# Neighbour sums and sort written out step by step, sums between the last node products, ten tiles of the first normalisation on ScalarE

## The chip, the cores and the metric

One Trainium2 chip, of which the kernel uses one core. The metric is the device time of one execution in microseconds (us), as the median of several runs; lower is better. A profiled execution stands beside it: one run of the same program taken by the hardware profiler, whose trace all rows below come from.

The engines are called by the names of the trace: PE (TensorE, matmul; PEld is its weight load), DVE (VectorE), ACT (ScalarE), POOL (GpSimd) and SP (SyncE, which only starts transfers here). Each runs its own instruction stream, in order, and waits on semaphores that the others raise. A small processor ahead of each engine, the sequencer, reads that stream: it carries out register and branch instructions itself and hands the rest to the engine's queue.

## The reference

Four updates of a node table `x` of 3,125 nodes by 256 values, each on the layer-normalised table:

```python
x = x + _L0_gnn_ref(_layernorm(x), src, dst, weight, bias)      # mean of h[src] over 50,000 edges, h = x @ W + b
x = x + _L0_ffn_ref(_layernorm(x)[None], ...)                   # graph attention on 32,768 edges picks 2 of 4 experts per node
x = x + _L1_gnn_ref(_layernorm(x), src, dst, edge_type_32, edge_weight1, bases, w_comp)   # 32 relations from 8 bases
x = x + _L1_ffn_ref(_layernorm(x)[None], Wr, br, W1, ...)       # mean of all nodes picks 2 of 8 experts, one choice for all
...
# _L1_ffn_ref: logits = jnp.mean(x, axis=1) @ Wr + br; softmax; scale by capacity; softmax; top_k; two expert MLPs; layernorm
```

All of it is float32. The last expert choice needs the mean over all nodes of the normalised table before any of its expert products can start.

## The kernel before, in words

Nodes are held as 25 tiles of 128 (`NT`), edges as 391 blocks of 128 (`EB`). The program is a row of blocks of code, one after the other.

**First normalisation and neighbour sums** (`sum_neighbours`). `normalise` (line 185) has DVE take the statistics of the 25 tiles, ACT a square root, and DVE then write all 25 normalised tiles `XN` (line 196). SP stores them to `xn_table` in five pieces of five tiles (line 603), and POOL begins to gather rows once all five have landed (line 615). Each gather (line 473) fetches the 128 source rows of one edge block; POOL keeps 16 blocks ahead of the sums at most (`LEAD_A`) and waits for PE in groups of four.

The sums run in 52 steps (`step`) of eight slots. In each step PE reads from tables in memory which ring place each slot's rows lie in and which gathers have to have landed (`registers` and `counts`, TENSOR_LOAD rows of line 123 and 131), and makes eight products of a one-hot matrix with the gathered rows (line 763) into four banks; DVE adds each bank to the node's sum (line 1148) and makes the next one-hot matrices (line 962).

Into these steps a second job is woven: a counting sort of the 32,768 attention edges. It uses whatever PE, DVE and ACT have free between the sums, and goes through four stretches:

- counting, 14 steps: written out on PE and DVE, a loop on ACT (line 674);
- two steps in which totals are made;
- bases, 5 steps (`BASED` to `PLACED`): a loop on PE (841), on DVE (1179) and on ACT (683);
- placing, 32 steps, one chunk of the sort in each (b = 0 to 31): on DVE b = 0 to 3 and 30, 31 are written out, the rest is a loop of two steps per turn (1192); on PE b = 0, 1 and b = 16, 17 are written out, b = 2 to 15 and 18 to 31 are two loops of seven turns (866, 871); on ACT b = 4 to 31 is a loop (693). Three more steps follow.

In a placing step, PE makes `equals` (781, 785), the places of the chunk before (`places_of`, 795 and 797) and the permutation of the one before that (804); ACT copies (652) and builds columns (662, 665); DVE carries values (1093), reads the places (1083 to 1088), makes tiles (1036), and at the step's end the one-hot rows of the next chunk (`hots`, line 1078), for which SP has loaded a row of digits (609). PE's `equals` of a step needs DVE's `hots` of the step before, so no engine can run more than about a step ahead.

Inside a loop the addresses and the values that a wait compares with depend on the turn, so each is worked out in registers by the sequencer; written out they are constants.

**Middle.** The update of the nodes, the attention, the experts and the sums over relations follow, none of them touched by the change.

**Last update** (`third_update`). PE makes the last four node products `z_ps` (line 2308, 16 products each); between them it turns (transposes, line 2301) the 21 tiles that are already normalised, seven after each of the first three node products (`SUMS`); ACT copies each turned tile out of one of two PSUM buffers (2269). DVE adds the products to `X` (2374), measures, and sums the turned tiles over the nodes (`node_sums`, 2369) in four groups: 7, 7, 7 and 4 tiles. The router of some 30 small DVE instructions (2398 to 2434) follows, then the transfers of the chosen experts' weights (SP, 2244), then the expert products (2330, 2342).

```python
SUMS = [range(0, 7), range(7, 14), range(14, NT - ZT), range(NT - ZT, NT)]     # line 2206, ZT is 4
```

## Time and profile before

| | us |
|---|---|
| median of 3 runs (lowest, highest) | 2281.04 (2280.89, 2281.67) |
| the profiled execution, its own time | 2285.36 |
| its span in the trace | 2283.6 |
| start to first gather | 0 to 47.33 |
| first gathers and counting | 47.33 to 212.00 |
| bases (5 steps) | 212.00 to 278.68 |
| placing and the last steps | 278.68 to 694.60 |
| node update, attention, experts | 694.60 to 1200, about |
| experts, sums over relations | 1200 to 2033, about |
| last node products and router | 2033.00 to 2092.00 |
| last experts, output | 2092.00 to 2283.60 |

Busy over the span: PE 1666.2 us (73%), DVE 1276.7 (56%), POOL 1076.5 (47%), ACT 712.2 (31%).

How to read it: start times are us from the start of the span. "issue" as a releaser means that the engine waited for nothing that the profile shows, and "remote" that what let it go has no engine's record beside it. A step's end is taken here as DVE's row of line 1078, which is made once per placing step.

### The profile page before, as it was taken

The numbers are of one execution on the slowest core, as the hardware profiler recorded it, in microseconds if no ns is written. First come the engines' busy times: TensorE is split into PE (matmuls) and PEld (weight loads), VectorE is DVE, ScalarE is ACT, GpSimd is POOL, SyncE is SP. The second block draws the span as 40 slices with busy tenths as digits, with TensorE's granted clock in tenths as the row PEclk, the third lists the DMA queues.
The fourth block names the chain that finished last, engine by engine and source line by source line (L and its number), as shares of the span: only waits on it lengthen the run. The fifth ranks groups of instructions, "written<-read, shape, count | busy, mean of one in ns | idle before, by whom it ended". The sixth has DMA issues, their size and how long they took to land. (4 is left out here: it accounts for less than half of the span.)

```text
span 2283.6 us, 32653 instructions
## 1 busy us (share of the span) xinstructions
PE 1666.2 (73%) x8780; PEld 1319.3 (58%) x8781; DVE 1276.7 (56%) x3698; ACT 712.2 (31%) x1566; POOL 1076.5 (47%) x1102
## 2 busy tenths in 40 slices
PE   2776566766777799999934646565756799996997
PEld 1444344444445577777723546555645699984786
DVE  7877777667677410222146636555656566656235
ACT  1001146555651222222204632232323233312222
POOL 1676666555660566666640065555555554300000
PEclk9987578788789799999966867777777799997999
DMA  5233233333332122232251543433333565611001
GB/s 165 78 89 92 73 98 104 96 104 103 101 97 74 29 70 70 69 91 70 76 158 8 177 129 117 133 118 118 116 112 114 166 219 197 201 37 42 0 1 57
DMA packets 165026, 226.82 MB, mean 99 GB/s; under 512 B 35764, under 2 KB 124118, under 8 KB 162070
## 3 DMA queue, kind: packets, MB, share of 16 engines
q0 software_dynamic: 47392, 105.58, 16.5%
q1 hardware_dynamic: 114176, 115.99, 15.7%
q10 hardware_dynamic: 3318, 3.59, 0.5%
q8 instruction: 63, 1.03, 0.2%
q14 instruction: 77, 0.63, 0.1%
HBM read 172.48 MB, written 105.03 MB: 122 GB/s over the span
## 5 line engine op out<-in xcount | busy, mean ns | idle before, releaser
L473 POOL DMA_INDIRECT edge_rows<-xn_table,edge_source x391 | 376.5, 963 | 402.2 <-ACT held L2111 177.6
L2123 PE MATMUL part<-coef,held 128*128 128x128 f32 x2368 | 400.8, 317 | 215.7 <-issue 181.0
L473 POOL DMA_INDIRECT shared_space<-xn_table,edge_source x391 | 402.4, 1029 | 277.8 <-issue 108.5
L2123 PEld LDWEIGHTS part<-coef,held 128*128 128x128 f32 x2368 | 371.4, 228 | 254.6 <-issue 199.3
L2161 DVE SCALAR_TENSOR_TENSOR window_sums<-window_sums,fine_keep,part 128x256 f32 x592 | 282.4, 477 | 295.9 <-remote 130.2
L763 PE MATMUL part<-shared_space,hot 128*128 x832 | 297.9, 495 | 123.9 <-issue 63.4
L2111 ACT ACTIVATE held<-edge_rows 128x256 f32 x592 | 213.9, 408 | 484.6 <-PE part L2123 228.3
L1490 POOL DMA_INDIRECT gall<-attention_table,attention_source x256 | 244.9, 957 | 132.5 <-issue 68.3
L763 PEld LDWEIGHTS part<-shared_space,hot 128*128 128x128 f32 x832 | 176.7, 239 | 194.2 <-issue 173.4
L1148 DVE TENSOR_TENSOR shared_space<-shared_space,part 128x257 f32 x416 | 174.6, 420 | 132.8 <-remote 43.5
L2148 DVE SCALAR_TENSOR_TENSOR coef<-iota,fine_target,slot_coefs 128x128 f32<-128x128 f32 x592 | 203.7, 346 | 6.8 <-PEq L1283 6.8
L1843 DVE TENSOR_TENSOR ys<-ps_of_attention,b 128x256 f32<-128x256 f32 x100 | 39.0, 419 | 299.3 <-PE ps_of_attention L1649 171.8
L1649 PE MATMUL ps_of_attention<-slot_coefs,hid 128*128 128x256 f32 x800 | 185.1, 388 | 18.5 <-DVE ys L1843 11.5
L1636 PE MATMUL ps_of_attention<-shared_space,W 128*128 128x320 f32 x640 | 181.6, 441 | 11.3 <-ACT hid L1532 8.5
L1649 PEld LDWEIGHTS ps_of_attention<-slot_coefs,hid 128*128 128x128 f32 x800 | 154.6, 194 | 47.5 <-DVE ys L1843 16.2
L2137 PE MATMUL z_ps<-bases,z 128*128 128x256 f32 x672 | 175.6, 383 | 1.3 <-issue 1.2
L1532 ACT ACTIVATE hid<-ps_of_attention,b 128x320 f32<-128x320 f32 x160 | 83.3, 527 | 266.5 <-PE ps_of_attention L1636 157.3
L1636 PEld LDWEIGHTS ps_of_attention<-shared_space,W 128*128 128x128 f32 x640 | 123.5, 194 | 64.7 <-ACT hid L1532 10.4
L662 ACT ACTIVATE sort_apart<-slot_iota,sort_col 128x256 bf16<-128x256 f32 x256 | 109.1, 496 | 45.9 <-DVEq L1089 34.1
L2137 PEld LDWEIGHTS z_ps<-bases,z 128*128 128x128 f32 x672 | 116.0, 193 | 10.3 <-issue 1.4
L2330 PE MATMUL h_ps<-XNT,V 128*128 128x320 f32 x320 | 90.1, 441 | 13.4 <-DMA V<-in_L_ffn_W 13.4
L2342 PE MATMUL y_ps<-window_sums 128*128 128x256 f32 x400 | 88.1, 379 | 0.5 <-DVE XN L2473 0.5
(467 smaller groups left out, 1926.4 us busy)
## 6 DMA issues: line engine op xcount, KB each, us to landing
basis_sums<-window_sums SPq DMA_DIRECT2D x74, 1024.0 KB
z<-basis_sums SPq DMA_DIRECT2D x21, 1024.0 KB
expert_rows<-ys SPq DMA_DIRECT2D x20, 640.0 KB
shared_space<-expert_rows SPq DMA_DIRECT2D x25, 512.0 KB, 4.7
W<-in_L_ffn_W SPq DMA_DIRECT2D x20, 512.0 KB
gall<-attention_digits SPq DMA_DIRECT2D x32, 256.0 KB
xn_table<-shared_space SPq DMA_DIRECT2D x10, 640.0 KB, 4.1
shared_space<-xn_table,edge_source POOLq DMA_INDIRECT x391
```

What stands on the lines that cost most here:

```text
L473: pool.indirect_dma_start(rows[:, b % ring, 0:D], None, table, bass.IndirectOffsetOnAxis(ap=esrc[:, b:b + 1].bitcast(U32), axis=0)).then_i ...
L662: nc.scalar.activation(apart[:, t, :], edges.slot_iota[:, 0:GT], ACT.Abs, bias=col[k][:, q * 4 + t:q * 4 + t + 1]).then_inc(apart_ready, 1)
L763: nc.tensor.matmul(part[:, n % BANKS, 0:D + 1], hot[n // HOT][:, n % HOT, :], rows[:, ds(at[n], 1), :].rearrange("p o d -> p (o d)"), star ...
L1148: V.tensor_tensor(to, to, part[:, n % BANKS, 0:D + 1], ALU.add).then_inc(added, 1)
L1490: pool.indirect_dma_start(gall[:, k, :], None, drams.table, at(att.source[:, k:k + 1])).then_inc(flights[i % FLIGHT], 16)
L1636: mm = nc.tensor.matmul(h_ps[:, n % BANKS_E, 0:HALF], W1[m % 2][:, c, f * P:(f + 1) * P], XNT[:, c, lo:lo + HALF], start=(c == 0), stop=(c ...
L1649: mm = nc.tensor.matmul(y_ps[:, (m * CT + t) % BANKS_E, :], hid[m % 2][:, f, t * P:(t + 1) * P], W2[:, m % EXPERTS, f, :], start=(f == 0), ...
L2111: nc.scalar.activation(held[k % DEEP][:, :], rows[:, ds(at[n], 1), :].rearrange("p o d -> p (o d)"), ACT.Copy).then_inc(copied, 1)
L2123: mm = nc.tensor.matmul(part[n][:, c * P:(c + 1) * P], held[n][:, c * P:(c + 1) * P], coef[n][:, :, :].rearrange("p b w -> p (b w)"), star ...
L2137: mm = nc.tensor.matmul(z_ps[:, t % 2, :], third.turned[t % AHEAD_Z][:, c * BASES + b, :], third.bases[:, b, c, :], start=(o == 0), stop=( ...
L2148: V.scalar_tensor_tensor(coef[k % DEEP][:, :, :], iota[:, 0:WIN].unsqueeze(1).to_broadcast([P, BASES, WIN]), fine.target[:, k:k + 1], coef ...
L2161: V.scalar_tensor_tensor(to, to, fine.keep[:, k:k + 1], part[k % DEEP].rearrange("p (k w) -> p k w", w=WIN), ALU.mult, ALU.add).then_inc(a ...
```

## The change

Four parts. (1) `normalise` makes tiles 0 to 14 on DVE; ACT makes tiles 15 to 24 as `x * root + off`, with `off` = minus mean times root from one more DVE instruction, and starts the stores of the last two pieces itself. (2) Every loop of the sums and the sort is written out, on PE, DVE and ACT. (3) In the last update, the turns stand singly between the 16 products of the second and the third node product, 11 and 10 of them, and `node_sums` has three groups, 11, 10 and 4 tiles; the first two are summed around the last node product's evictions. (4) In the router the comparison of indices `earlier` is made before the logits are waited for.

```diff
-    for t in range(NT):
+    link(dve.scalar_tensor_tensor(off, aggr[:, :, 0], -1.0, root, ALU.mult, ALU.mult))
+    for t in range(X_OWN):
         dve.tensor_scalar(XN[:, t, :], X[:, t, :], aggr[:, t, 0:1], root[:, t:t + 1],
...
-X_FIRST = 8
+X_FIRST, X_OWN = 8, 15
...
             for lo, hi in zip(CUTS, CUTS[1:]):
+                if hi > X_OWN:
+                    break
                 sp.wait_ge(xn_ready, hi)
...
+            act.wait_ge(xn_ready, 1)
+            for t in range(X_OWN, NT):
+                nc.scalar.activation(XN[:, t, :], X[:, t, :], ACT.Identity, bias=off[:, t:t + 1], scale=root[:, t:t + 1]).then_inc(act_made, 1)
+            for lo, hi in zip(CUTS, CUTS[1:]):
+                if lo >= X_OWN:
+                    act.wait_ge(act_made, 1 + hi - X_OWN)
+                    act.dma_start(table.rearrange("(t p) d -> p t d", p=P)[:, lo:hi, :], XN[:, lo:hi, :]).then_inc(xn_out, 16)
...
-            with act.Fori(0, PAIRS - 1) as ii:
+            for ii in range(PAIRS - 1):
...
-            with act.Fori(0, NT // CT) as w:
+            for w in range(NT // CT):
...
-            with act.Fori(2, CHUNKS_S // 2) as ii:
+            for ii in range(2, CHUNKS_S // 2):
...
-            with pe.Fori(BASED, PLACED) as i:
+            for i in range(BASED, PLACED):
                 step(i)
...
-            with pe.Fori(1, HALFWAY) as ii:
+            for ii in range(1, HALFWAY):
...
-            with pe.Fori(HALFWAY + 1, CHUNKS_S // 2) as ii:
+            for ii in range(HALFWAY + 1, CHUNKS_S // 2):
...
-            with dve.Fori(BASED, PLACED) as i:
-                link.enter(i - BASED, 2 * CT)
+            for i in range(BASED, PLACED):
                 step(i, parts=basing(i - BASED))
-                link.leave(PLACED - BASED)
...
-            with dve.Fori(2, CHUNKS_S // 2 - 1) as ii:
-                link.enter(ii - 2, 2 * PLACING)
+            for ii in range(2, CHUNKS_S // 2 - 1):
...
-        SUMS = [range(0, 7), range(7, 14), range(14, NT - ZT), range(NT - ZT, NT)]
+        SUMS = [range(0, 11), range(11, NT - ZT), range(NT - ZT, NT)]
...
-                mm.then_inc(z_ready, 1)
-                if t + ZT - NT < len(SUMS) - 1:
-                    for n in SUMS[t + ZT - NT]:
-                        turn(n)
+                    if n == len(third.products) - 1:
+                        mm.then_inc(z_ready, 1)
+                    group = t - (NT - ZT) - 1
+                    if 0 <= group < len(SUMS) - 1 and n < len(SUMS[group]):
+                        turn(SUMS[group][n])
...
+                if n == ZT - 1:
+                    node_sums(len(SUMS) - 2)
                 dve.wait_ge(z_ready, t + 1)
...
-                if 0 < n < len(SUMS) - 1:
-                    node_sums(n - 1)
+                if n == ZT - 2:
+                    node_sums(0)
...
-            for g in range(len(SUMS) - 2, len(SUMS)):
-                node_sums(g)
+            node_sums(len(SUMS) - 1)
```

What the change does to the instruction streams, at three places. Line numbers above 190 are up to ten higher in the changed program.

**PE, start of a placing step** (lines 763, 773: the sums; 795, 805 and 797, 807: the places). Before, in the loop:

```order
L758 ISA
L762 REGISTER_ALU
L763 ISA
L763 MATMUL part<-shared_space,hot 128x257
L762 REGISTER_ALU
L763 ISA
L763 MATMUL part<-shared_space,hot 128x257
L790 ISA
L795 ISA
L795 MATMUL word_ps<-sort_bases,gall 128x50
L797 MATMUL word_ps<-shared_space,edge_rel 128x25
L795 ISA
```

Now:

```order
L773 ISA
L773 MATMUL part<-shared_space,hot 128x257
L773 ISA
L773 MATMUL part<-shared_space,hot 128x257
L805 MATMUL word_ps<-sort_bases,gall 128x50
L807 MATMUL word_ps<-shared_space,edge_rel 128x25
L805 MATMUL word_ps<-sort_bases,gall 128x50
```

The register rows for the waits and for the address of each place product are gone; the row that sets the ring address of each sum stays. A placing step is 65 rows on PE before and 39 now.

**DVE, start of a placing step** (1148, 1158: the adds; 1093, 1103: the carry). Before:

```order
L1192 ISA
L123 TENSOR_LOAD coarse_tile
L1145 REGISTER_ALU
L1146 REGISTER_ALU
L1148 ISA
L1148 TENSOR_TENSOR shared_space<-shared_space,part 128x257
L1145 REGISTER_ALU
L1146 REGISTER_ALU
L1148 ISA
L1148 TENSOR_TENSOR shared_space<-shared_space,part 128x257
L1100 REGISTER_ALU
L1093 ISA
```

Now:

```order
L123 TENSOR_LOAD coarse_tile
L1158 ISA
L1158 TENSOR_TENSOR shared_space<-shared_space,part 128x257
L1158 ISA
L1158 TENSOR_TENSOR shared_space<-shared_space,part 128x257
L1103 TENSOR_SCALAR edge_norm<-sort_iota,sort_row,shared_space 128x128 x8
L1158 ISA
```

Here too only the rows that depend on data stay; a placing step is 65 rows on DVE before and 28 now.

**PE, the last node products** (2308, 2314) **and the turns between them** (2301, 2307). Before:

```order
L2308 MATMUL z_ps<-bases,window_sums 128x256 x16
L2301 MATMUL xnt_ps<-ident,XN 128x128 x14
L2308 MATMUL z_ps<-bases,window_sums 128x256 x16
L2301 MATMUL xnt_ps<-ident,XN 128x128 x14
L2308 MATMUL z_ps<-bases,window_sums 128x256 x16
```

Now:

```order
L2314 MATMUL z_ps<-bases,window_sums 128x256 x17
L2307 MATMUL xnt_ps<-ident,XN 128x128 x2
L2314 MATMUL z_ps<-bases,window_sums 128x256
L2307 MATMUL xnt_ps<-ident,XN 128x128 x2
L2314 MATMUL z_ps<-bases,window_sums 128x256
```

The three blocks of seven turns are gone, and one turn (two transposes) stands behind each single product instead.

## Rows read from the trace of the kernel before

**Rows 1.** The page, costliest groups: busy, mean ns of one, idle before:

```profile
L473 POOL DMA_INDIRECT shared_space<-xn_table,edge_source x391 | 402.4, 1029 | 277.8 <-issue 108.5
L2111 ACT ACTIVATE held<-edge_rows 128x256 f32 x592 | 213.9, 408 | 484.6 <-PE part L2123 228.3
```

**Rows 2.** Windows: length, busy of PE, PEld, DVE, ACT, POOL, PEclk, DMA, GB/s:

```profile
84.00:196.00 112.00, 81.98 (x441) 50.69 (x441) 87.42 (x173) 11.65 (x32) 82.05 (x75) 0.83 0.31 91
...
305.48:658.73 353.25, 249.49 (x1450) 173.43 (x1450) 253.32 (x755) 200.98 (x344) 209.73 (x216) 0.83 0.35 102
...
480.84:500.43 19.59, 15.70 (x100) 11.53 (x100) 17.14 (x54) 12.17 (x20) 12.26 (x13) 0.88 0.38 108
```

**Rows 3.** Waits in 300 to 692 us (POOL: 40 to 692): total, times, longest:

```profile
PE part L763 <- issue: 39.1, 38, 2.2
...
DVE shared_space L1148 <- remote: 43.2, 17, 5.8
...
POOL shared_space L473 <- PE part L763: 99.6, 38, 9.3
```

**Rows 4.** Timeline of DVE, the row that ends a placing step:

```profile
305.48 0.48 DVE L1078 TENSOR_SCALAR gall<-gall,lane 128x1024 bf16<-128x1024 bf16 x1
...
480.84 0.48 DVE L1078 TENSOR_SCALAR gall<-gall,lane 128x1024 bf16<-128x1024 bf16 x1
...
490.84 0.48 DVE L1078 TENSOR_SCALAR gall<-gall,lane 128x1024 bf16<-128x1024 bf16 x1
...
500.43 0.48 DVE L1078 TENSOR_SCALAR gall<-gall,lane 128x1024 bf16<-128x1024 bf16 x1
...
658.73 0.48 DVE L1078 TENSOR_SCALAR gall<-gall,lane 128x1024 bf16<-128x1024 bf16 x1
```

**Rows 5.** Timeline of one stall in the placing loop, PE and DVE:

```profile
403.07 0.61 PE L781 MATMUL equal_ps<-sort_earlier,sort_ident 128*128 128x512 bf16 x1 [1.91 <-issue]
...
406.18 0.99 DVE L1148 TENSOR_TENSOR shared_space<-shared_space,part 128x257 f32 x2 [5.12 <-remote]
```

**Rows 6.** Timeline of DVE, the first add of three steps of the bases loop:

```profile
236.32 0.42 DVE L1148 TENSOR_TENSOR shared_space<-shared_space,part 128x257 f32 x1 [1.45 <-issue]
...
248.02 0.42 DVE L1148 TENSOR_TENSOR shared_space<-shared_space,part 128x257 f32 x1 [1.44 <-issue]
...
268.10 0.42 DVE L1148 TENSOR_TENSOR shared_space<-shared_space,part 128x257 f32 x1 [1.44 <-issue]
```

**Rows 7.** DMA queue of instructions, whole span and 300 to 692 us: packets, MB, share:

```profile
q8 instruction: 63, 1.03, 0.2%
...
q8 instruction: 4, 0.07, 0.1%
```

**Rows 8.** Timeline of the first normalisation: start, length, engine, line:

```profile
33.59 8.16 DVE L196 TENSOR_SCALAR shared_space<-X,aggr,root 128x256 f32<-128x256 f32 x25
35.32 6.82 SPq L603 DMA_DIRECT2D xn_table<-shared_space  x5
...
47.33 1.14 POOL L473 DMA_INDIRECT shared_space<-xn_table,edge_source  x1 [44.36 <-DMA xn_table<-shared_space]
```

**Rows 9.** Timeline of the last node products:

```profile
2042.90 0.60 PE L2301 MATMUL xnt_ps<-ident,XN 128*128 128x128 f32 x4
...
2046.04 7.07 PE L2308 MATMUL z_ps<-bases,window_sums 128*128 128x256 f32 x32
...
2054.17 1.99 DVE L2369 TENSOR_REDUCE node_parts<-XNT 128x2 f32<-128x1792 f32 x1
...
2056.09 7.07 PE L2308 MATMUL z_ps<-bases,window_sums 128*128 128x256 f32 x32
...
2077.41 3.03 DVE L2369 TENSOR_REDUCE node_parts<-XNT 128x2 f32<-128x1792 f32 x2
2078.53 0.81 ACT L2269 ACTIVATE XNT<-xnt_ps 128x256 f32<-128x256 f32 x2 [0.41 <-PE xnt_ps L2301]
```

**Rows 10.** Timeline of PE, the one long wait in the written-out steps:

```profile
205.07 3.79 PE L763 MATMUL part<-shared_space,hot 128*128 x8 [5.70 <-issue]
```

More of the change, by code:

```diff
@@ L182, in measure, with normalise @@
     link.note(dve.bn_aggr(aggr[:, t, :], stats[:, t, :]))
-def normalise(dve, link, X, XN, stats, aggr, var, root, tmp, var_ready, std_ready, n, xn_ready, measured):
+def normalise(dve, link, X, XN, stats, aggr, var, root, tmp, off, var_ready, std_ready, n, xn_ready, measured):
     for t in range(measured, NT):
@@ L503, in sum_neighbours @@
         stats, aggr = edges.stats, sb("aggr0", [P, NT, 2])
-        var, root, tmp = (sb(f"{n}0", [P, NT]) for n in ("var", "root", "tmp"))
+        var, root, tmp, off = (sb(f"{n}0", [P, NT]) for n in ("var", "root", "tmp", "off"))
         ends, windows = sb("block_ends", [P, 3, EC], I32), sb("block_windows", [P, 2, 3, EC], I32)
@@ L566, in sum_neighbours @@
         xn_ready, xn_out, pads_out, digits_out = (sem(n) for n in ("xn_ready", "xn_out", "pads_out", "digits_out"))
-        src_turned, src_ready, last_ready, number_ready, start_ready = (
-            sem(n) for n in ("src_turned", "src_ready", "last_ready1", "number_ready", "start_ready"))
+        src_turned, act_made, last_ready, number_ready, start_ready = (
+            sem(n) for n in ("src_turned", "act_made", "last_ready1", "number_ready", "start_ready"))
         sel_ready, words_ready, words_used = sem("sel_ready"), sem("words_ready"), sem("words_used")
@@ L630, in _ @@
             act.wait_ge(src_turned, 1)
-            nc.scalar.activation(esrc[:, :], word_ps[:, 0, :], ACT.Copy).then_inc(src_ready, 1)
+            nc.scalar.activation(esrc[:, :], word_ps[:, 0, :], ACT.Copy).then_inc(act_made, 1)
             act.wait_ge(digits_turned, 1)
@@ L748, in _ @@
             pe.wait_ge(sel_ready, 2)
-            pe.wait_ge(src_ready, 1)
+            pe.wait_ge(act_made, 1)
             pe.wait_ge(words_used, 1)
@@ L890, in _ @@
             dve.wait_ge(edges.x_in, 16 * (NFULL // X_FIRST))
-            normalise(dve, link, X, XN, stats, aggr, var[:, :], root[:, :], tmp[:, :], var_ready, std_ready, 1, xn_ready, X_FIRST)
+            normalise(dve, link, X, XN, stats, aggr, var[:, :], root[:, :], tmp[:, :], off[:, :], var_ready, std_ready, 1, xn_ready, X_FIRST)
             dve.wait_ge(last_ready, 1)
@@ L2394, in softmax @@
                 link(V.tensor_scalar(x, sm[:, :], tmp[:, 0:1], None, ALU.mult))
+            e_of = lambda x: x.unsqueeze(2).to_broadcast([P, E8, E8])
+            o_of = lambda x: x.unsqueeze(1).to_broadcast([P, E8, E8])
+            link.note(V.tensor_tensor(earlier[:, :, :], o_of(iota[:, 0:E8]), e_of(iota[:, 0:E8]), ALU.is_lt))
             dve.wait_ge(logits_ready, 1)
@@ L2410, in _ @@
             softmax(lg[:, :], 2)
-            e_of = lambda x: x.unsqueeze(2).to_broadcast([P, E8, E8])
-            o_of = lambda x: x.unsqueeze(1).to_broadcast([P, E8, E8])
             link.note(V.tensor_tensor(larger[:, :, :], o_of(lg[:, :]), e_of(lg[:, :]), ALU.is_gt))
-            link.note(V.tensor_tensor(equal[:, :, :], o_of(lg[:, :]), e_of(lg[:, :]), ALU.is_equal))
-            link(V.tensor_tensor(earlier[:, :, :], o_of(iota[:, 0:E8]), e_of(iota[:, 0:E8]), ALU.is_lt))
+            link(V.tensor_tensor(equal[:, :, :], o_of(lg[:, :]), e_of(lg[:, :]), ALU.is_equal))
             link(V.tensor_tensor(equal[:, :, :], equal[:, :, :], earlier[:, :, :], ALU.mult))
```

3 lines of the change are left out of this document (1 added, 2 removed).

## The prediction

> **What bounds the kernel now.** The chain that ended last only reaches back over the last tenth of the span, so I read the stages by windows, then the waits, then the timeline.
>
> The stage that the change is mostly about is the placing, from 278.68 to 694.60 us. The reader is to see in its window [rows 2] that over 353.25 us no engine is full: PE 249 us, DVE 253 us, POOL 210 us. The window runs from the end of one placing step to the end of the 29th after it (305.48 and 658.73) [rows 4], so a step takes 353.25 / 29 = 12.18 us. The waits say what fills the gaps [rows 3]: 39.1 us in which PE waited for nothing the profile shows before a sum, 43.2 us in which DVE waited for "remote" before an add, and 99.6 us of POOL waiting for PE's sums. One stall shows how they hang together [rows 5]: PE idles 1.91 us before its `equals` with no releaser, and DVE's next add starts 5.12 us late.
>
> Two of these steps are different. The kernel before has placing steps b = 16 and 17 written out on PE, while DVE and ACT are inside their loops. Their ends are at 490.84 and 500.43, after 480.84 [rows 4]: 10.00 and 9.59 us, with DVE 87% busy [rows 2]. The same work costs 2.4 us less where PE's sequencer has no addresses and wait values to work out. I conclude that **PE's register work is what makes the looped steps slow**, a mechanism inferred from two steps.
>
> In the bases stage, the first adds of three successive steps stand at 236.32, 248.02 and 268.10 [rows 6]: 11.7 us for one turn of DVE's loop and 20.1 for the next, with the same instructions. The counting stage has no loop on PE or DVE. Over 112 us POOL issued 75 gathers [rows 2]; with 108.5 / 391 = 0.28 us of issue gap each [rows 1] that is 82 + 21 = 103 us of 112, so POOL bounds it.
>
> **The change part by part.**
>
> *Placing written out.* 26 rows per step go on PE, 37 on DVE. What bounds a step next? On DVE and PE together, the two written-out steps: 9.6 to 10.0 us. On POOL: 216 gathers in 29 steps [rows 2] are 7.45 per step, at (402.4 + 108.5) / 391 = 1.31 us each [rows 1], 9.7 us. Both floors lie close together, so each one's jitter falls on the other, and I take 10.2 us: 29 × (12.18 − 10.2) = 57 us. Best case 9.6 us, 75 us; the worst that a row gives is POOL at its price in the counting stage, 112 / 75 = 1.49 us, 7.45 × 1.49 = 11.1 us per step, 31 us. The last placing step and the three steps behind it, still paced by PE's loop when they start, give two more such differences: 4 us (2 to 5).
>
> *Bases written out.* The gain is the slow turn: 20.1 − 11.7 = 8.4 us [rows 6]; I take 8. It may be chance that one turn was slow, so the lower bound is 0. The 1.44 us ahead of each step's first add is a read of a table from memory, which stays.
>
> *ACT's loops written out.* ACT is 57% busy in placing (201 of 353 us [rows 2]) and 10% in counting; POOL covers it there. Nothing. If that cover went, ACT's part is the copy of the counts, off PE's path by one chunk.
>
> *More code to fetch.* The written-out stretch adds 24 placing steps' code on PE, at 1450 / 29 = 50 records each of PE and PEld [rows 2], and four bases steps: some 2,900 instructions. The whole program's 17,500 such records came in 63 packets of q8 [rows 7], which by its size is PE's queue, so 280 each; that makes 10 or 11 packets more. I cost them at nothing: the counting stage runs such code and is bound by POOL. Nearest row for a price: the longest written-out wait, 5.70 us [rows 10], though DVE's long reduction stands there too.
>
> *A rule on this point.* In 300 to 692 us q8 moved 4 packets [rows 7], while PE went 14 times through its two placing loops: the loops were not fetched anew. The Trainium skill, "Runtime: NRT & Kernel Launch", section "Instruction fetch mechanics", says that a taken branch to code outside the two pages held forces a fetch and a stall, and gives that as a reason to unroll. By this rule alone the placing loops would have at most 4 such stalls to give back, and the sum would end where the first rival does; the trace does not bear it out as the cause here.
>
> *First normalisation.* DVE's 25 tiles take 8.16 us [rows 8], 0.33 each; ten fewer and one small instruction more free DVE 3.0 us earlier. ACT makes its ten beside DVE, at 0.41 us for a 128x256 tile [rows 1]: 4.1 us from about 34.3, ready at 38.5 instead of 41.75. Behind that tile came the last store and 5.6 us to the first gather (41.75 to 47.33) [rows 8]. ACT starts two stores one behind the other after its tiles, about 1 us of that lost (SP's five take 6.8 us with their waits). First gather about 2.2 us earlier, and with POOL as the bound of counting this carries: 2.2 us (0 to 3).
>
> *Last node products.* A node product takes 7.07 us, and the next starts 10.05 us after it [rows 9]: 3.0 us for seven turns, because each pair of turns waits for ACT's copies. Three blocks: 9 us. Two turns without waits take 0.60 us on PE [rows 9], partly latency; I take 0.23 each, 21 × 0.23 = 4.8 us, the copies hidden behind the products. Gain 4.2 us (2.5 to 4.8). The turns now wait for nothing new: the 21 tiles are normalised while the first product runs. DVE's sums grow: 7 tiles 1.99 us [rows 9], so 11 and 10 take 3.1 and 2.8; with the 1.2 us of eviction and statistics ahead of them that is 7.1 us beside the last product's 7.07, so they just fit, and half a microsecond is the risk. The sum of tiles 14 to 20 leaves the end of the chain, but gains nothing: the last group's sum could only begin when ACT's last copy ended, at 78.53 + 0.81 = 79.34, and the pair ended at 80.44 [rows 9]; one sum of four tiles after 79.34 ends there too. What is late next is that copy.
>
> *Router.* One instruction of about 0.2 us leaves the chain: 0.2 us.
>
> **Sum.** 57 + 4 + 8 + 2 + 4 + 0.2 = 76 us (rounded from 57.4, 4, 8, 2.2, 4.2, 0.2). The profiled execution took 2285.36 us with a span of 2283.6, 0.19% above the median of the runs, so the difference is taken from the median: 2281 − 76 = **2205 us** (a profile of it would show about 2209). The stages behind the sums start from a common point at 694.6 and move as they are.
>
> **The rivals.**
>
> *The loops cost next to nothing, chance 0.10.* The stalls come from the tables that PE and DVE read in each step and from the landings of gathers, all of which stay; b = 16 and 17 were lucky. For it: DVE's looped and written-out steps do the same engine work. Against it: the "remote" waits stand nowhere in the written-out stretches. Time: only 2.2 + 4.2 + 0.2 are gained, 2274 us. The Trainium skill, "Advanced Engine Details and Errata", section "Control Flow Timing", gives 51 ns for a branch and 108 ns for a compare and branch; by this, 19 turns of PE's loops are an estimated 2 us, and the sum would be 2272.
>
> *POOL becomes the bound at its counting price, 0.12.* POOL's gathers took 1.09 us each where DVE was 78% busy (82.05 / 75) and 0.97 where it was 72% busy [rows 2]; a denser DVE may slow them again. 11.1 us per step: 31 + 2 + 6 + 6 = 45 us, or 2236 us.
>
> *The straight code is fetched too slowly, 0.04; slower than before.* Each of the 11 further packets holds PE up by 5.7 us [rows 10], 63 us, and everyone behind it. It decides only if the loops give back little too: 2281 − 7 + 63 = 2337 us. With my gains for the loops it would take 7 us per packet to cancel them. Against it: the placing steps 16 and 17 and the counting stage are such code.
>
> *Better than the forecast, 0.04:* all placing steps at 9.6 us or below, under 2186 us.
>
> **How the numbers follow.** The forecast has 0.70. Its best bounds together (75, 5, 8.4, 3, 4.8) reach 2185 us; the POOL rival with no gain from the bases reaches 2243. The range of 2186 to 2243 holds both cases, 0.82. Faster by over 0.2% (4.6 us, about what a measurement of this kernel can tell from no change): all cases but the fetch rival and a part of the first, 0.94. Within 0.2%: 0.02. Slower: 0.04.
>
> **What would show it.** A profile after should have placing steps 9.6 to 10.5 us apart, no "remote" waits of DVE's adds above 2 us, q8 packets up by about 11, five bases steps all near 11.7 us, the first gather near 45 us, the last node products 9.2 to 9.6 us apart with no gap of 3 us, and a placing stage of about 355 us for 416. The prediction is wrong if steps stay at 12 us (then not PE's registers), if POOL's waits for PE vanish and its gathers lengthen (POOL rival), or if PE shows waits of several us that coincide with q8 packets.

## The result, and the profile after

The changed kernel takes 2258.7 us (median of 4 runs, 2255.6 to 2259.4), the kernel before beside it 2280.97 us (2280.6 to 2281.7): ratio 0.9886, 95% interval 0.9870 to 0.9902. It is faster by 22 us where 76 were forecast, and lies outside the range of 2186 to 2243 us.

The profiled execution of the changed kernel took 2255.6 us, the fastest of its runs (that of before took 2285.4, above its own runs), so the two profiles stand 30 us apart where the medians stand 22. I therefore compare stages, and take the spread of a stage from the profiles of the experiments. Windows of the changed kernel (columns as in [rows 2]), the counting stage and 29 placing steps:

```profile
84.00:196.00 112.00, 84.16 (x436) 52.88 (x434) 89.26 (x171) 10.71 (x30) 81.73 (x76) 0.80 0.33 93
292.85:636.93 344.08, 235.68 (x1450) 165.73 (x1450) 252.63 (x755) 201.66 (x344) 209.12 (x216) 0.88 0.36 105
```

29 placing steps now take 344.08 us, 11.86 us each, where [rows 2] had 12.18 and the forecast 10.2. The waits of the same window name what stays:

```profile
PE equal_ps L791 <- ACT edge_rel L662: 51.3, 19, 4.2
ACT edge_rel L662 <- remote: 48.9, 19, 5.8
...
DVE shared_space L1158 <- remote: 38.1, 16, 5.2
POOL shared_space L474 <- remote: 34.9, 14, 2.7
```

The "remote" waits that were to vanish are there: 16 before DVE's adds, 38.1 us, against 17 and 43.2 in [rows 3], which look at a somewhat longer stretch. The other parts moved more nearly as forecast, all but the first gather. The code grew by 12 packets ([rows 7] had 63), and ScalarE made its part of the first normalisation beside VectorE:

```profile
q8 instruction: 75, 1.23, 0.2%
```

```profile
36.71 1.08 ACT L641 ACTIVATE shared_space<-X,off,root 128x256 f32<-128x256 f32 x2
36.87 2.34 DVE L197 TENSOR_SCALAR shared_space<-X,aggr,root 128x256 f32<-128x256 f32 x7
37.33 0.40 ACTq L645 DMA_DIRECT2D xn_table<-shared_space  x1
...
39.78 0.37 ACTq L645 DMA_DIRECT2D xn_table<-shared_space  x1
```

```profile
48.70 1.39 POOL L474 DMA_INDIRECT shared_space<-xn_table,edge_source  x1 [45.73 <-DMA xn_table<-shared_space]
```

VectorE is free at 39.2 us instead of 41.75, but ScalarE takes 0.51 us a tile, its last store is issued at 39.78, and the first gather comes at 48.70, later than the 47.33 of [rows 8].

In the last update the turns stand between products. VectorE's adds for the second and the third of the last four node products are 9.1 us apart, where they were 10.05 before, and the sums of 11 and 10 tiles just fit before the last one:

```profile
2026.79 0.42 DVE L2383 SCALAR_TENSOR_TENSOR X<-z_ps,X 128x256 f32<-128x256 f32 x1 [8.23 <-PE z_ps L2314]
2035.91 0.42 DVE L2383 SCALAR_TENSOR_TENSOR X<-z_ps,X 128x256 f32<-128x256 f32 x1 [8.01 <-PE z_ps L2314]
2036.93 5.78 DVE L2376 TENSOR_REDUCE node_parts<-XNT 128x2 f32<-128x2816 f32 x2
2042.81 0.42 DVE L2383 SCALAR_TENSOR_TENSOR X<-z_ps,X 128x256 f32<-128x256 f32 x1
```

**One freeze in the written-out code.** These are rows of five timelines of the changed kernel in one placing step: TensorE, SyncE, GpSimd, and ScalarE and VectorE, which wait:

```profile
302.62 0.19 PE L807 MATMUL word_ps<-shared_space,edge_rel 128*128 128x25 bf16 x1
303.39 0.39 PE L791 MATMUL equal_ps<-sort_earlier,sort_ident 128*128 128x512 bf16 x1 [0.57 <-DVE gall L1088]
303.61 0.39 PE L795 MATMUL equal_ps<-gall 128*128 128x128 bf16 x4
303.84 1.96 PE L773 MATMUL part<-shared_space,hot 128*128 x8
309.77 0.61 PE L791 MATMUL equal_ps<-sort_earlier,sort_ident 128*128 128x512 bf16 x1 [3.97 <-ACT edge_rel L662]
...
308.89 0.32 SPq L612 DMA_DIRECT2D gall<-attention_digits  x1
...
302.51 1.24 POOL L474 DMA_INDIRECT shared_space<-xn_table,edge_source  x1 [0.31 <-issue]
304.06 0.95 POOL L474 DMA_INDIRECT shared_space<-xn_table,edge_source  x1 [0.30 <-DMA shared_space<-xn_table,edge_source]
305.31 0.95 POOL L474 DMA_INDIRECT shared_space<-xn_table,edge_source  x1 [0.30 <-issue]
306.56 0.94 POOL L474 DMA_INDIRECT shared_space<-xn_table,edge_source  x1 [0.30 <-issue]
309.80 0.95 POOL L474 DMA_INDIRECT shared_space<-xn_table,edge_source  x1 [2.29 <-remote]
...
309.02 0.69 ACT L662 ACTIVATE edge_rel<-equal_ps,sort_minus 128x512 bf16<-128x512 f32 x1 [3.49 <-remote]
309.12 0.42 DVE L1158 TENSOR_TENSOR shared_space<-shared_space,part 128x257 f32 x1 [2.84 <-remote]
```

TensorE's last place product (L807) ends at 302.81. SyncE's load of the next digits waits for that product's signal alone, and is issued at 308.89, 6.1 us later. ScalarE waits for the signal of `equals`, recorded as done at 304.0, until 309.02; VectorE waits for sums recorded from 303.84 on until 309.12; the three go on within 0.25 us of each other. By its records TensorE has not stopped working: its signals are late, and come together. The semaphore records in the same trace say so directly: TensorE's updates for L807 and L795 and its next four for the sums stand at 308.87, 308.94, 308.98, 309.03, 309.07 and 309.11, while VectorE's updates are recorded all through, at 304.53 to 306.29. I call such a stretch a freeze. Meanwhile GpSimd issues four gathers one behind the other, then needs sums itself and stops at 307.50; 1.4 us later the signals come. In a step without a freeze:

```profile
353.54 0.19 PE L807 MATMUL word_ps<-shared_space,edge_rel 128*128 128x25 bf16 x1
...
353.76 0.32 SPq L612 DMA_DIRECT2D gall<-attention_digits  x1
...
351.56 0.94 POOL L474 DMA_INDIRECT shared_space<-xn_table,edge_source  x1 [0.30 <-issue]
354.32 0.94 POOL L474 DMA_INDIRECT shared_space<-xn_table,edge_source  x1 [1.82 <-PE part L773]
```

Here the signal is taken 0.03 us after the product, and GpSimd has been quiet for 1.2 us. In each of the two profiles a load of SyncE waits for 30 of the place products, and I set these 60 against the gathers around them: 14 signals came at once, and in 12 of these GpSimd's last gather had ended about 1.2 us or more before; 46 came 1.4 to 8.8 us late, and in all of these a gather was in issue or had ended at most 0.3 us before. This gave **theory A**: signals of TensorE are held while gathers follow each other without a gap, until about when the last of them has landed. The rival is the forecast's own, **F**: TensorE's register work in loops costs 2 us a step.

### The profile page after: what moved, and what is told of

Read it like the earlier page. It is cut to its first block and busy times, and to the rows that moved or that the text cites. A ratio compares the mean times of both kernels' runs of the same rounds, so it can differ in the third digit from the quotient of the medians.

```text
span 2253.8 us, 30851 instructions
## 1 busy us (share of the span) xinstructions
PE 1663.8 (74%) x8780; PEld 1321.2 (59%) x8780; DVE 1272.7 (56%) x3687; ACT 716.8 (32%) x1576; POOL 1072.9 (48%) x1102
## 5 line engine op out<-in xcount | busy, mean ns | idle before, releaser
L474 POOL DMA_INDIRECT shared_space<-xn_table,edge_source x391 | 396.3, 1013 | 261.1 <-issue 110.8
L773 PE MATMUL part<-shared_space,hot 128*128 x832 | 291.9, 492 | 107.4 <-issue 53.5
L1642 PE MATMUL ps_of_attention<-shared_space,W 128*128 128x320 f32 x640 | 187.2, 448 | 17.3 <-issue 12.6
L1655 PE MATMUL ps_of_attention<-slot_coefs,hid 128*128 128x256 f32 x800 | 178.8, 382 | 8.9 <-DVE ys L1849 7.7
L672 ACT ACTIVATE sort_apart<-slot_iota,sort_col 128x256 bf16<-128x256 f32 x256 | 109.1, 496 | 64.5 <-DVEq L1099 47.0
```

Source lines behind the costliest of these rows:

```text
L474: pool.indirect_dma_start(rows[:, b % ring, 0:D], None, table, bass.IndirectOffsetOnAxis(ap=esrc[:, b:b + 1].bitcast(U32), axis=0)).then_i ...
L773: nc.tensor.matmul(part[:, n % BANKS, 0:D + 1], hot[n // HOT][:, n % HOT, :], rows[:, ds(at[n], 1), :].rearrange("p o d -> p (o d)"), star ...
L1642: mm = nc.tensor.matmul(h_ps[:, n % BANKS_E, 0:HALF], W1[m % 2][:, c, f * P:(f + 1) * P], XNT[:, c, lo:lo + HALF], start=(c == 0), stop=(c ...
L1655: mm = nc.tensor.matmul(y_ps[:, (m * CT + t) % BANKS_E, :], hid[m % 2][:, f, t * P:(t + 1) * P], W2[:, m % EXPERTS, f, :], start=(f == 0), ...
```

## The experiments

The measure I use for a run's placing stage is the row of the digits' comparison, whose first and last start are 31 steps apart. The kernel before has 278.7 to 658.7, 380.0 us; the changed kernel 370.6:

```profile
L1088 DVE TENSOR_SCALAR gall<-gall,lane x32: 478/481/547, 266.3 to 636.9; 128x1024 bf16<-128x1024 bf16 x32
```

**The loops alone.** The kernel before with its seven loops written out, nothing else:

```diff
-            with pe.Fori(1, HALFWAY) as ii:
+            for ii in range(1, HALFWAY):
```

(and so for the six others).

> The kernel before with only its seven counted loops of the neighbour sums and the sort written out (the first normalisation and the last update as before). The changed kernel gained 22 us in all, 19 us of it by the end of the sort and 3 us in the last update. Theory A (the written-out loops brought the gain of the first stage): 2281 - 19 = 2262 us, 2259 to 2266, with a placing step near 11.9 us. Rival B (the gain of the first stage comes mostly from the first normalisation and its earlier chain of words, or from the phase in which gathers and steps meet): 2270 us or more.

Measured: 2262.1 us (2260.1 to 2268.5), ratio 0.9898 (0.9862 to 0.9934). The total is what the first of the two theories expected, but not where it comes from: the placing takes 378.3 us, almost as before. The bases take 50.9 us from first to last scan for 61.8, and 14 us lie in the edge sums (694.7 for 709.1), a stage that no part of the change touches. Over all profiles of the two kernels that stage has 687 to 709 us: the total of one kernel carries some 10 us that belong to nothing in the change.

**More and less credit for the gathers.**

```diff
-LEAD_A, LEAD_T, TURNS = 16, 16, 8
+LEAD_A, LEAD_T, TURNS = 12, 12, 8
```

(24, 24 in the second.)

> The changed kernel with both gather streams allowed to run 12 blocks ahead and not 16. Theory A (signals of TensorE that follow the place products are held while GpSimd goes on issuing gathers, and come through about 1.0 to 2.1 us after its last one, so what ends a freeze is that the gathers run out of credit): less credit ends the freezes sooner, but only if a group of four less is issued inside one; the freezes of 5.5 us (three gathers issued inside) become 2 to 4 us and the placing step falls from 11.9 to 11.0 to 11.5 us, the whole 2235 to 2255 us. Rival B (gathers that land late hold the step): less lead makes every landing later for TensorE, the step grows to 12.5 us or more and the whole to 2275 us or more. Rival C (the freeze has nothing to do with the gathers): 2256 to 2262 us.

> The changed kernel with both gather streams allowed to run 24 blocks ahead and not 16. Theory A (held until the gathers run out of credit): more credit gives longer freezes, where the stream has used it; the placing step 12.0 to 12.6 us, the whole 2262 to 2290 us. Rival B (gathers that land late hold the step): more lead removes late landings, step 10.2 to 11 us, the whole 2215 to 2240 us. Rival C (no connection): 2256 to 2262 us.

Measured: 12 ahead 2247.2 us, ratio 0.9821 (0.9789 to 0.9853); 24 ahead 2278.2 us, 0.9970 (0.9950 to 0.9990). The order is theory A's, and B (late landings) is refuted, but the mechanism was not seen: the placing takes 379.2 and 375.9 us, and the freezes stay. A likely reason, not tested by itself: a group of four starts when sums arrive, just before the place products, at any lead. With 24 the loss stands in the counting stage (first scan of the bases at 224.1 us for 211.7) and in the edge sums (711.7 us for 702.5).

**Groups of two and of eight.**

```diff
-GROUP, FLIGHT, BEFORE = 4, 4, 2
+GROUP, FLIGHT, BEFORE = 2, 4, 3
```

(8, 4, 2 with 24 ahead in the second.)

> The changed kernel with gathers issued in groups of two and not of four, 16 ahead as before (a ring of 43 blocks and not 44, so that the longer table fits; landings told three groups later and not two). Theory A (TensorE's signals after the place products are held until about 1 to 2 us after GpSimd's last gather): GpSimd asks for credit after every second gather, so at most one or two gathers are issued inside a freeze; freezes of 5.5 us become 2 to 3.5 us, the placing step falls from 11.9 to 10.5 to 11.3 us, and the edge sums gain too: the whole 2215 to 2245 us. Rival B (the freeze is independent of the gathers): freezes stay at 5.5 us, the step at 11.9 to 12.2 us, and GpSimd has a credit wait more each 2.5 us: 2255 to 2275 us.

> The changed kernel with gathers in groups of eight, 24 ahead (the same slack to the landings told as with fours and 16). Theory A: a group that starts at the place products goes on for 10 us, so freezes of 8 to 11 us appear, the placing step is 13 to 15 us and the whole 2290 to 2340 us, against the run with fours and 24 ahead. Rival B (freezes independent of the gathers' groups): freezes at 5.5 us, step 11.9 to 12.3 us, whole 2260 to 2285 us.

Measured: twos 2258.6 us, ratio 0.9854 (0.9823 to 0.9886), placing 380.6 us; eights 2328.9 us, 1.0166 (1.0137 to 1.0195), placing 402.9 us. For the eights the waits in 305 to 660 us:

```profile
ACT edge_rel L662 <- remote: 81.5, 20, 11.6
DVE shared_space L1158 <- remote: 55.7, 16, 11.3
```

Eights behave as A says: the longest freezes have 11.3 and 11.6 us, and it is the only kernel slower than before (with fours and 24 ahead the ratio was 0.9970), with 728.2 us in the edge sums too. Twos do not: freezes after the place products shorten, but as many microseconds come back elsewhere in the step. How the credit is dealt out moves the freezes; it does not remove them.

**Half the gathers.** In blocks 160 to 351 every second gather is not issued, and nobody waits for it:

```diff
+            if left_out(b):
+                continue
             pool.indirect_dma_start(
```

> The changed kernel in which every second gather of blocks 160 to 351 is left out (nobody waits for its landing), so that GpSimd needs 5 us of a placing step and not 10; the sums of neighbours are then of stale rows. Theory A (signals held while gathers are issued): most place products meet no gather in issue or one of two, the freezes of 5.5 us vanish from these steps, which come to 10.0 to 10.6 us: some 20 steps by 1.5 us, whole 2220 to 2235 us. Rival B (the freeze is TensorE's own or the instruction fetch's): steps stay at 11.9 us and the whole at 2255 to 2260 us.

> The kernel before, loops and all, with every second gather of blocks 160 to 351 left out. Theory A (the stalls of the looped steps are the held signals, the loops themselves cost 0.1 to 0.4 us a step): placing steps 10.0 to 10.4 us, whole 2281 - 24 x 1.9 and some more = 2220 to 2240 us. Rival F, the forecast's own (TensorE's register work in the loops costs about 2 us a step): steps 11.9 to 12.2 us as before, whole 2270 to 2285 us.

Measured: changed kernel 2204.5 us, ratio 0.9618 (0.9586 to 0.9649); kernel before 2219.1 us, 0.969 (0.963 to 0.975). The rows of the digits' comparison, of the changed kernel with half the gathers:

```profile
L1091 DVE TENSOR_SCALAR gall<-gall,lane x32: 478/482/542, 268.8 to 589.2; 128x1024 bf16<-128x1024 bf16 x32
```

and of the kernel before, loops and all, with half of them:

```profile
L1081 DVE TENSOR_SCALAR gall<-gall,lane x32: 479/481/547, 279.2 to 600.1; 128x1024 bf16<-128x1024 bf16 x32
```

320.4 and 320.9 us: **with and without loops the placing takes the same time**. In the changed kernel 21 of the 24 steps from the fourth on took 9.87 to 9.96 us; the looped ones alternate between 9.6 to 9.8 and 10.0 to 10.2. This is the floor that the forecast read from steps 16 and 17, and the loops are not what stands above it. F, 2 us in every looped step, is refuted. Of the 30 place signals 24 (changed kernel) and 22 (before) now come at once, for 5 and 9 with all gathers, and between the fourth step and the end of the left-out blocks none is over 1 us late. The clock does not set the step either: the steps that start at 344.82 and at 503.72 both took 9.87 us, one at a granted clock of 1.00 (its upper level, 2.4 GHz) all through, the other at a mean of 0.70, partly at each level. One rival is still open here: with half the gathers GpSimd has time to spare as well.

**GpSimd busy with something else.** As before, but each left-out gather is replaced by four clearings of 128x176 elements.

```diff
             if left_out(b):
+                for _ in range(4):
+                    nc.gpsimd.memset(common.scratch[:, :], 0.0).then_inc(common.paused, 1)
```

> As the run with half the gathers left out (blocks 160 to 351), but where a gather is left out GpSimd clears 176 elements a partition four times instead, so that it is kept busy without moving data. Theory A1 (TensorE's signals are held by the traffic of gathers that follow each other without a gap): the time of the run with half the gathers stands as far as GpSimd's clearing allows: placing steps 9.9 to 10.3 us, whole 2200 to 2215 us. Theory A2 (they are held by a busy GpSimd, whatever it does): the freezes come back, step 11.5 us or more, whole 2235 to 2260 us.

Measured: 2238.5 us, ratio 0.9795 (0.9735 to 0.9855). The total lies in the interval of A2 (2235 to 2260) and not in that of A1 (2200 to 2215), so it speaks for A2; the trace has to tell what it is made of. No wait of the placing stretch (305 to 590 us) has "remote" as its releaser, and with GpSimd at work before, at and behind the place product SyncE's load follows at once (product recorded 400.18 to 400.37, load 400.40):

```profile
399.48 1.17 POOL L479 MEMSET scratch_rows<- 128x176 f32 x4
400.92 0.95 POOL L482 DMA_INDIRECT shared_space<-xn_table,edge_source  x1 [0.27 <-POOL scratch_rows L479]
401.87 1.25 POOL L479 MEMSET scratch_rows<- 128x176 f32 x4
```

Here 28 of the 30 place signals come at once, and the two late ones stand outside the blocks concerned. Most steps take 9.9 to 10.5 us, but two take 11.2 and 11.7 and five take 14.2 to 15.7 us. In those TensorE waits for GpSimd's word that gathers have landed (42.5 us in 15 waits over the stretch) and GpSimd for its credit; how the two come to wait for each other I have not followed further. So a busy GpSimd alone holds no signal, which A2 needed, and the time lost is not in freezes.

**Half the bytes.** As many gathers, each bringing 128 elements of a row and not 256:

```diff
-            pool.indirect_dma_start(rows[:, b % ring, 0:D], None, table,
+            pool.indirect_dma_start(rows[:, b % ring, 0:D // 2 if halved else D], None,
+                                    table.rearrange("r (h d) -> (r h) d", h=2) if halved else table,
```

> The changed kernel in which the gathers of blocks 160 to 351 bring 128 elements of a row and not 256 (from other rows of the table, the other half of a block stale): as many gathers and rows, half the bytes. If the bytes in flight hold TensorE's signals: the freezes vanish as with half the gathers, step 9.9 to 10.4 us, whole 2205 to 2225 us. If it is the number of gathers or rows that follow each other: freezes and step as in the changed kernel, 11.8 to 12.2 us, whole 2253 to 2265 us.

Measured: 2257.4 us, ratio 0.9887 (0.9847 to 0.9926), placing 372.4 us, 13 "remote" waits of VectorE's adds in 305 to 590 us with 32.2 us (14 and 33.7 in the changed kernel), and 4 of 30 place signals at once. It is not the bytes. Whether it is the number of gathers or of rows in them this run does not tell, as both stayed.

**The credit again, with the changed kernel beside it.**

> The changed kernel itself, beside the two runs that follow, since the kernel before lay between 2273 and 2298 us in the last runs and the ratios alone compare: ratio 0.985 to 0.990 by every theory.

> The changed kernel with 12 blocks ahead and not 16, beside the changed kernel on the same chip. Its first run gave a ratio of 0.982 where the changed kernel had 0.989, but its profile showed no shorter freezes in the placing stage (step 12.2 us). If less credit helps: 0.3 to 0.8% below the changed kernel. If the first run was the spread of runs: within 0.3% of it.

> The changed kernel with gathers in groups of two and 8 ahead (landings told two groups later). Theory A (signals held as long as gathers follow each other): GpSimd has credit for at most a few gathers at any time, so the long freezes go, and the placing step is 10.6 to 11.4 us: whole 2220 to 2245 us. Rival (the lead is then too short for the landings, some 2.5 to 3 us behind the issue): each pair is waited for, step 12.5 us or more, edge sums slower too, whole 2280 us or more.

Measured: changed kernel 2254.1 us, ratio 0.9869 (0.9835 to 0.9904); 12 ahead 2247.9 us, 0.9849 (0.9817 to 0.9882); pairs with 8 ahead 2274.8 us, 0.9956 (0.9935 to 0.9976). That 12 ahead beats the changed kernel stays unsettled: both of its profiles show shorter edge sums (698.9 and 696.6 us, changed kernel 702.5 and 705.5), but a third profile of the changed kernel, on another chip, has 687.4, and the intervals overlap. Pairs with 8 ahead are worse in the placing (394.9 us) and better in the edge sums (680.6 us); a kernel with short credit in the edge sums alone was not tried.

**Parts undone.** The first normalisation, then the last update:

```diff
-X_FIRST, X_OWN = 8, 15
+X_FIRST, X_OWN = 8, NT
```

> The changed kernel with all 25 tiles of the first normalisation made by VectorE and all five stores issued by SyncE, as before the change (the multiplication for the offsets stays). Theory A (the first part brought nothing: the first gather came 1.4 us later than before, though the chain of words started earlier): within 3 us of the changed kernel, 2255 to 2262 us, first gather near 47 us. Rival B (the earlier chain of words was worth its 2.5 us): 2261 to 2264 us.

> The changed kernel with the last update as it was before (four groups of node sums, turns after each node product, the router's comparison in its old place). Expected from the two profiles (61.7 us from the last edge product of TensorE to its first product of the experts before, 59.9 after): the stretch is 2 to 4.5 us longer than in the changed kernel, the whole 2258 to 2265 us. Rival: no difference (under 1 us), 2255 to 2260 us.

Measured: all tiles on VectorE 2265.6 us, ratio 0.9873 (0.9839 to 0.9907); old last update 2256.0 us, 0.9873 (0.9808 to 0.9937). The first total lies above both of its intervals, the second at the lower end of the rival's, beside kernels before of 2290 and 2286 us; totals cannot tell parts of 5 us, the profiles can. VectorE's first add stands at 75.2 us in the first of these and at 71.1 in the changed kernel, 67.9 to 71.1 in every run of these chips with ScalarE's tiles and 73.9 to 75.4 in every run without, though the first gather comes no earlier with them. From TensorE's last edge product to its first product of the experts it is 64.8 us with the old last update (65.6 and 64.5 in two other runs that had it, 62.8 and not 61.7 in the kernel before) and 59.9 in the changed kernel (57.6 to 60.0 in all that have the new one).

**Placing loops back, and bases loops back.** In the changed kernel:

```diff
-            for ii in range(1, HALFWAY):
+            with pe.Fori(1, HALFWAY) as ii:
```

(with the second loop of TensorE, those of ScalarE and VectorE), and for the bases `with pe.Fori(BASED, PLACED) as i:` with its two companions.

> The changed kernel with the counted loops of the placing steps back on TensorE, VectorE and ScalarE; bases, counting, first normalisation and last update stay changed. Theory A (the loops of the placing steps cost next to nothing, the gathers set the step): from the last scan of the bases to the last sum within 6 us of the changed kernel, whole 0 to 4 us above it, 2254 to 2264 us. Rival F (the forecast's term): 57 us back, 2305 to 2320 us.

> The changed kernel with the counted loops of the five bases steps back on TensorE, VectorE and ScalarE. Theory (these loops are the ones that were worth writing out: from the first to the last scan 61.8 us in the kernel before and 57.4 in its run with half the gathers, 50.8 to 52 in every run with them written out): that stretch goes back to 57 to 62 us, whole 2260 to 2268 us. Rival (that gain too is given back at the gathers): 2254 to 2260 us.

Measured: 1999.6 us, ratio 0.9931 (0.9919 to 0.9944), and 2009.0 us, 0.9976 (0.9967 to 0.9986), beside a kernel before of **2014.3 us** (2011 to 2018). These two ran on a chip on which the same kernel is 270 us faster. Their totals cannot be set against expectations made for the other chips; their traces can. On that chip all 30 place signals come at once in both runs, 24 and 19 of them with a gather in issue; here is one, in the kernel with the placing loops back:

```profile
325.35 0.19 PE L807 MATMUL word_ps<-shared_space,edge_rel 128*128 128x25 bf16 x1
...
325.57 0.32 SPq L612 DMA_DIRECT2D gall<-attention_digits  x1
...
325.40 0.99 POOL L474 DMA_INDIRECT shared_space<-xn_table,edge_source  x1 [0.30 <-issue]
```

The placing takes 311.5 us, its gathers as long as elsewhere:

```profile
L474 POOL DMA_INDIRECT shared_space<-xn_table,edge_source x391 | 403.0, 1031 | 175.8 <-issue 106.8
```

```profile
L1088 DVE TENSOR_SCALAR gall<-gall,lane x32: 479/481/539, 249.8 to 561.3; 128x1024 bf16<-128x1024 bf16 x32
```

So GpSimd issues every gather and the steps still take 10 us: what was open behind the run with half the gathers is settled, its spare time is not needed. The clock is no rival: over the placing it was 0.89 and 0.85 in these two and 0.87 in the changed kernel. The written-out placing steps of the other run take 316.6 us there: where nothing is frozen, the loops are even 5 us the faster. The bases take 50.9 us written out and 52.1 looped. As no changed kernel stood beside these two, the next pair has both:

> The changed kernel itself on the same chip as the run that follows, because the last two runs came to a chip on which the kernel before takes 2014 us and not 2285 us and the freezes are all but absent, so that they have no changed kernel beside them. On a chip of the first kind: ratio 0.985 to 0.990 and some 110 us of held place signals. On a chip of the second kind: no freezes, written-out placing steps of 10.0 us, ratio 0.994 to 0.997 (the placing loops back gave 0.9931 there with steps of 9.8 us).

> The changed kernel with the counted loops of the placing steps back, beside the changed kernel. Theory A (those loops cost nothing; without freezes the looped steps are even 0.17 us shorter than the written-out ones): on a chip of the first kind within 4 us of the changed kernel, on one of the second kind 3 to 7 us below it. Rival F (the forecast's term): 40 to 57 us above it on either.

Measured, on a chip with freezes: changed kernel 2232.2 us, ratio 0.9896 (0.9874 to 0.9918); placing loops back 2240.4 us, 0.9940 (0.9921 to 0.9959). Undoing the written-out placing costs 8 us, of which I had expected 0 to 4 and the forecast 57; its placing stretch has 379.0 us for 366.7. Keeping these loops does not beat the changed kernel here.

What these loops do cost stands in the rows of their register instructions (min, median and longest in ns). The kernel with the placing loops back is the same program in both of its runs; first the chip with freezes, then the one without, for TensorE (L772) and VectorE (L1155):

```profile
L772 PEldq ALU_OP  x224: 3/32/721, 281.2 to 647.2; - x112
L1155 DVEq ALU_OP  x78: 6/40/703, 311.1 to 620.6; - x78
```

```profile
L772 PEldq ALU_OP  x224: 32/32/42, 269.4 to 565.1; - x112
L1155 DVEq ALU_OP  x78: 40/40/64, 296.1 to 543.9; - x78
```

On the chip with freezes some of them take 0.7 us and not 0.03 or 0.04. I counted those above 0.3 us in the placing: 55 on TensorE and 33 on VectorE in this kernel, 49 and 27 in the kernel before, 10 and 4 in the kernel before with half the gathers, none in any kernel whose placing is written out, and none on the other chip. In the bases loops VectorE has 10 of them in the kernel before, none on the other chip. So register work does cost something here, but only where single instructions of it are slowed, and never the 2 us in each step. Why they are slowed is not shown.

## Why the prediction was wrong, step by step

- **Placing written out, 57 us and 4 behind it: this is the step that failed.** It rested on the sentence that "PE's register work is what makes the looped steps slow, a mechanism inferred from two steps". Measured on chips with freezes: 380.0 and 379.0 us looped, 366.7 to 378.3 written out (six profiles of the changed kernel and its nearest relatives, mean 372.5), so about 7 us, and 12 us in the one pair on the same chip; with half the gathers 0.5 us; without freezes −5 us. What keeps the steps at 12 us is TensorE's signals, late while gathers follow each other, with and without loops. (Of the 99.6 us of POOL's waits that it also read into this stage, taken from 40 to 692 us, 71.6 lie in 300 to 692.) Steps 16 and 17 were fast because no long freeze lay in them: the late signal before step 16 had come at 480.07, before the step began, the next place product ends at 490.89, and its signal came 2.7 us later. And they were not alone. Of the steps that are looped on all three engines, b = 6, 13, 24 and 25 took 10.2, 9.6, 10.1 and 9.9 us in the same profile of the kernel before; this is step 13, looped, from end to end:

```profile
442.02 0.48 DVE L1078 TENSOR_SCALAR gall<-gall,lane 128x1024 bf16<-128x1024 bf16 x1
...
451.60 0.48 DVE L1078 TENSOR_SCALAR gall<-gall,lane 128x1024 bf16<-128x1024 bf16 x1
```

The forecast had the right outcome among its rivals, at 0.10 ("b = 16 and 17 were lucky", the stalls come from things "which stay"), though with table reads and landings as the cause. It dismissed it because the "remote" waits "stand nowhere in the written-out stretches". That holds for VectorE's adds in two steps; ScalarE, in the counting stage of the kernel before (75 to 212 us), which is written out on TensorE, has seven of them:

```profile
ACT slot_coefs L645 <- remote: 21.3, 7, 5.7
```

- **Bases, 8 us: held in size, on chips with freezes.** 61.8 us from first to last scan before (57.4 in its run with half the gathers, which leaves these steps alone), 50.8 to 52.0 in the runs with fours: 6 to 11 us. In the changed kernel the steps take 11.24 us each from first add to first add, where the forecast had 11.7. The slow turn was no property of the loop alone: on the chip without freezes the looped bases cost 1.2 us. The forecast gave no cause for it, so that its size came out is in part luck.
- **More code, nothing: held.** 12 packets for 10 or 11, and near none of them does TensorE wait more than 1.6 us without a releaser. By the rule in the Trainium skill's "Runtime: NRT & Kernel Launch", "Instruction fetch mechanics", unrolling had at most 4 stalls to give in the placing; the 4 packets and the 7 us agree with that better than with my 57, though no row shows such a stall at any of the 4.
- **First normalisation, 2.2 us by an earlier first gather: right sign, wrong way.** The first gather came later in most runs (47.5 to 48.9 us, without ScalarE's tiles 47.3 to 47.6). ScalarE needs 0.585 us for a tile and starts one each 0.50 us, where the forecast took 0.41, and its stores are late. What is gained, 3 to 7 us at VectorE's first add, comes by VectorE's own earlier chain of small instructions to TensorE's first sum.
- **Last node products, 4.2 us, router 0.2: held.** The third product took 9.1 us, which lies just below the forecast's 9.2 to 9.6, and the stretch is 3 to 8 us shorter (57.6 to 60.0 for 62.8 to 65.6), 2.9 us between the first two profiles. The router's part was not measured by itself.
- **The sum.** 6 to 11 (bases), 7 (placing), 3 to 7 and 3 to 8 us make 19 to 33 us; measured were 22, and the edge sums move by more than the spread of any one part.

## What to carry to other kernels

When two steps of a stage are fast, list the time of every step first: here four looped ones were as fast. Then set every difference beside them, also in what other engines do at that moment, before choosing the one that the change removes. Several engines that freeze and go on together point to late signals of the one they all wait for: compare the end of the producer's row with the start of a consumer that waits for nothing else, and look at what was in flight in between. The cheapest test takes the suspected load away in both versions of the code, here half the gathers, which said in two runs what the total of any single part could not.

## What the runs showed of the hardware

On five chips the kernel before took 2249 to 2298 us, and TensorE's signals came up to 8.8 us late in the two first profiles while indirect gathers followed each other 1.25 us apart. On the sixth it took 2014 us with the same gathers (1031 ns each) and none of 60 place signals held in two profiles: the placing stretch was 312 to 317 us where the other kernels with gathers in fours had 367 to 380, the stage between the sums 562 where the changed kernel had 629, the edge sums 595 where it had 702. Its mean granted clock over the execution was 0.89 to 0.90 and theirs 0.84 to 0.86; over the placing alone the two kinds overlap (0.85 and 0.89 there, 0.80 to 0.87 elsewhere). Half the gathers, or gathers 2.4 us apart with GpSimd busy between them, cleared the placing steps of long freezes; half the bytes did not. On the chips with freezes, single register instructions inside the loops of TensorE and VectorE took up to 0.7 us (one 1.4 us); in the written-out bases and placing steps, and on the sixth chip, none took over 0.2 us. What holds the signals inside the chip, why it starts mostly at the place products, why register instructions are slowed, and what differs in the sixth chip stay open; no row of the profile names it. Gathers that follow each other are thus a part of the cause on five chips, and not enough for it on the sixth.
